# A Trainium2 decoder layer: a cap moved from VectorE to GpSimd, a residual in two halves, bias copies spread, and a query ahead of statistics

## The reference

```python
# attention: R, K, V are linear layers of a mix of the previous and the next token (width 1024)
e  = jnp.exp(jnp.clip(W + K, -20.0, 10.0))          # W = -relu(time_decay) * (t_remaining)
past_attention = jnp.cumsum(e * V, axis=1)
past_energy = jnp.cumsum(e, axis=1)
eu = jnp.exp(jnp.clip(U + K, -20.0, 10.0))
A = shift(past_attention) + eu * V
B = shift(past_energy) + eu
out = (jax.nn.sigmoid(R) * (A / B)) @ Wo.T + bo
# cross attention on ctx
Q = query @ Wq.T + bq ; K = key @ Wk.T + bk ; V = value @ Wv.T + bv
weights = jax.nn.softmax((Q @ K.T + score_matrix) / jnp.sqrt(32.0), axis=-1)
out = (weights @ V) @ Wo.T + bo
```

## Time and profile before

| | us |
|---|---|
| median of 3 runs | 1376.91 |
| lowest, highest | 1374.55, 1377.23 |
| the profiled execution | 1377.34 |
| its span (first to last instruction) | 1375.3 |

### The profile page before, as it was taken

The page is one execution under the profiler, slowest core; times in us unless marked ns, Lnnn a source line. Parts: engine busy times, 40 slices in busy tenths (PEclk is TensorE's granted clock), DMA queues, the critical chain, the costliest instruction groups (busy, mean ns, idle before and its releaser), DMA issues. The chain is left out here.

```text
span 1375.3 us, 19352 instructions
## 1 busy us (share of the span) xinstructions
PE 1327.4 (97%) x6330; PEld 1098.3 (80%) x6330; DVE 1090.5 (79%) x1782; ACT 813.5 (59%) x1555; POOL 634.0 (46%) x558
## 2 busy tenths in 40 slices
PE   5899999999999999999999999999999899999998
PEld 4777887887888878878886778888888778888886
DVE  6999989889899898898988776655555677777774
ACT  5875666656666666666665464444446366666664
POOL 4665344343443433434434544444445455555552
PEclk9999999999999999999999999999999999999999
DMA  9010101001001010010050354444443312222212
GB/s 349 9 30 2 61 31 50 13 31 61 13 17 61 31 58 3 31 61 0 1 222 1 138 210 168 150 146 153 166 147 120 104 59 92 91 91 91 92 62 92
DMA packets 54539, 113.92 MB, mean 83 GB/s; under 512 B 2768, under 2 KB 7120, under 8 KB 52560
## 3 DMA queue, kind: packets, MB, share of 16 engines
q1 hardware_dynamic: 54480, 113.22, 23.2%
HBM read 88.05 MB, written 25.17 MB: 82 GB/s over the span
## 5 line engine op out<-in xcount | busy, mean ns | idle before, releaser
L818 POOL TENSOR_TENSOR a_ss<-a_ss,a_eu 128x512 f32<-128x512 f32 x64 | 82.7, 1293 | 281.4 <-DVE a_ss L630 281.4
L612 DVE SCALAR_TENSOR_TENSOR bank<-bank,k_or_row 128x510 f32<-128x510 f32 x192 | 132.8, 692 | 56.3 <-ACT k_or_row L494 53.3
L823 POOL TENSOR_TENSOR a_sv<-a_sv,a_euv 128x512 f32<-128x512 f32 x64 | 82.8, 1294 | 119.0 <-DVE a_sv L647 119.0
L494 ACT ACTIVATE k_or_row<-bank 128x512 f32<-128x512 f32 x192 | 113.8, 593 | 5.7 <-PE bank L82 0.5
L514 ACT ACTIVATE bank<-bank,a_nbr 128x510 f32<-128x510 f32 x64 | 42.3, 661 | 123.0 <-DVE bank L612 123.0
L401 PE MATMUL bank<-a_wo_hi,a_y_hi 128*128 128x512 f32 x256 | 100.4, 392 | 0.0
L401 PE MATMUL bank<-a_wo_hi,a_y_lo 128*128 128x512 f32 x256 | 99.7, 389 | 0.0
L401 PE MATMUL bank<-a_wo_lo,a_y_hi 128*128 128x512 f32 x256 | 99.6, 389 | 0.0
L1510 POOL TENSOR_TENSOR b_cx_lo<-b_cx,b_cx_hi 128x512 fp32r<-128x512 f32 x32 | 40.6, 1299 | 113.2 <-ACT b_cx_hi L1205 113.2
L827 POOL TENSOR_TENSOR a_y_lo<-a_yy,a_y_hi 128x512 fp32r<-128x512 f32 x64 | 85.6, 1337 | 3.6 <-ACT a_y_hi L537 3.6
L526 ACT ACTIVATE bank<-a_ss 128x512 f32<-128x512 f32 x64 | 38.7, 604 | 74.8 <-DVE a_ss L653 74.8
(11 more groups left out here) (246 smaller groups left out, 4719.4 us busy)
## 6 DMA issues: line engine op xcount, KB each, us to landing
xres<-in_x SPq DMA_DIRECT2D x8, 1024.0 KB, 5.3
x_after_attention<-xres SPq DMA_DIRECT2D x8, 1024.0 KB, 4.3
xin<-x_after_attention SPq DMA_DIRECT2D x8, 1024.0 KB, 5.6
b_ct<-in_ctx_t SPq DMA_DIRECT2D x8, 1024.0 KB, 6.5
b_cx<-in_ctx SPq DMA_DIRECT2D x8, 1024.0 KB, 7.7
xres<-x_after_attention SPq DMA_DIRECT2D x8, 1024.0 KB, 5.7
x_after_cross<-xres SPq DMA_DIRECT2D x8, 1024.0 KB, 4.4
xin<-x_after_cross SPq DMA_DIRECT2D x8, 1024.0 KB, 5.5
```

Source lines behind the costliest of these rows:

```text
L494: sc.activation(u3[:, :, 1:], ps[m][:, :, :], ACT.Copy, scale=MIX[m]).then_inc(left[m], 1)
L612: ve.scalar_tensor_tensor(out=ps[m][:, :, 0:T - 1], in0=ps[m][:, :, 1:T], scalar=1.0 - MIX[m], in1=u3[:, :, 0:T - 1], op0=ALU.mult, op1=AL ...
L818: gp.tensor_tensor(ss3[:, :, 0:T], ss3[:, :, 0:T], eu[:, :, :], ALU.add).then_inc(b_done, 1)
L823: gp.tensor_tensor(sv3[:, :, 0:T], sv3[:, :, 0:T], euv[:, :, :], ALU.add).then_inc(a_done, 1)
```

## The change

Five edits, all in the order of programs or in which engine does a piece of work; no operation is added to the computation.

1. The cap of eu leaves VectorE's `clip` and becomes `clip_own` on GpSimd. VectorE's `weigh_own` now waits for it, and changes places with `mix("r")`.
2. On GpSimd `y_rest` of the group before moves from behind `above` to the front of the group, ahead of `clip_own`.
3. The residual's four additions become two after c = 1 and two in c = 2, between `refine` and `mix("v")`.
4. The bias broadcasts of the last tile are made one each after c = 4, 5 and 6, the two small ones after c = 6.
5. In the cross pass, for the first tile only, ScalarE splits the query high before the context, and VectorE splits the query's rest before and between the statistics of tile 2.

```diff
             def clip(g):
-                ve.tensor_scalar(eu[:, :, :], eu[:, :, :], CLIP_LO, CLIP_HI, ALU.max, ALU.min).then_inc(eu_clip, 1)
                 dve.wait_ge(e_exp, g + 1)
                 ve.tensor_scalar(ee3[:, :, 1:], ee3[:, :, 1:], CLIP_LO, CLIP_HI, ALU.max, ALU.min).then_inc(e_clip, 1)
...
             def weigh_own(g, c):
 
                 dve.wait_ge(edge_v, g + 1)
+                dve.wait_ge(eu_clip, g + 1)
                 wait(dve, a_done, g)
...
-            def wide_biases():
-
-                dve.wait_ge(sh.bias_in, 32)
-                dve.wait_ge(proj["v"], (NT - 1) * HC + KC)
-                for j, b in enumerate((1, 2, 0)):
-                    ve.tensor_copy(sh.bwide[:, j, :].rearrange("p (k r) -> p k r", k=KC),
-                                   sh.bcol[:, b, :].unsqueeze(2).to_broadcast([P, KC, P])
-                                   ).then_inc(bwide_done, 1)
+            def wide_bias(j):
+
+                if j == 0:
+                    dve.wait_ge(sh.bias_in, 32)
+                    dve.wait_ge(proj["v"], (NT - 1) * HC + KC)
+                ve.tensor_copy(sh.bwide[:, j, :].rearrange("p (k r) -> p k r", k=KC),
+                               sh.bcol[:, (1, 2, 0)[j], :].unsqueeze(2).to_broadcast([P, KC, P])
+                               ).then_inc(bwide_done, 1)
+
+            def dot_biases():
+
...
                     if back:
                         refine(g - 1)
+                    if c == 2 and not is_first(i):
+                        residual(i - 1, (2, 3))
                     mix("v", g)
                     clip(g)
                     scan_e(g)
+                    mix("r", g)
                     weigh_own(g, c)
-                    mix("r", g)
                     weigh(g, c)
                     scan_ev(g)
...
                     if c == 1 and not is_first(i):
-                        residual(i - 1, range(SUB))
-                    if is_last(i) and c == HC - 2:
-                        wide_biases()
+                        residual(i - 1, (0, 1))
+                    if is_last(i) and KC <= c < KC + 3:
+                        wide_bias(c - KC)
+                    if is_last(i) and c == KC + 2:
+                        dot_biases()
...
+            def clip_own(g):
+                if isinstance(g, int) and g == 0:
+                    pool.wait_ge(eu_exp, 1)
+                gp.tensor_scalar(eu[:, :, :], eu[:, :, :], CLIP_LO, CLIP_HI, ALU.max, ALU.min).then_inc(eu_clip, 1)
+
...
                         rstd_of(i + 1)
+                    if c > 0 or not is_first(i):
+                        pool.wait_ge(eu_exp, g + 1)
+                        y_rest(g - 1, (c - 1) % HC)
+                    clip_own(g)
                     below(g)
                     above(g)
-                    if c > 0 or not is_first(i):
-                        y_rest(g - 1, (c - 1) % HC)
...
                 for s in range(SUB):
                     exponent(i, s)
-                if ahead:
+                if is_first(i):
+                    q_high(1, 0)
+                    q_high(1, 1)
+                    for k in range(KC):
+                        context_high(1, k)
+                elif ahead:
                     context_high(i + 1, 0)
...
-                if ahead:
+                if is_first(i):
+                    move_rq(1)
+                    q_rest(1, 0)
+                    statistics(2, (0, 1))
+                    q_rest(1, 1)
+                    statistics(2, (2, 3))
+                    dve.wait_ge(st_done, 3 * SUB)
+                    aggregate()
+                elif ahead:
                     move_rq(i + 1)
                     statistics(i + 2)
```

## The result

The changed kernel takes **1476.55 us** (median of 4 runs, 1476.05 to 1476.69) against 1376.73 us for the kernel before on the same chip: a ratio of **1.073**, 95% interval 1.0716 to 1.0743. The forecast was 1435 us with a range up to 1470: right in sign and in the wait it named (before weigh_own), 42 us too small, and, as experiment 8 shows, with the memory going to VectorE and GpSimd in the other order than forecast.

What follows compares the result with a forecast made beforehand. VectorE's round bounds attention, TensorE following with little slack. Rounds +71.2, stretched caps −4.7, residual −5.7, bias −2.8, cross tile +0.3 make +58.3 on 1376.9: 1435 us, range 1395 to 1470.

Steps and rivals of the forecast that it cites:

- About this sum and no more: Attention: relieving VectorE can win only about TensorE's 23 waits for the weighting e·V, 14.4 us in all.
- X: Duration of the cap of eu on GpSimd: 0.94 us taken, 0.77 and 1.30 as ends.
- Rival 3: Cap of eu: two operations per element cost GpSimd twice, X near 1.85, +2.0 us a round, 1492 us; chance 0.03.
- Times 63: Attention: a plain round grows from 10.60 to 11.73 us, +1.13, counted for 63 rounds: +71.2 us.
- rival 1: Attention: y_rest gets the memory before the scan, +0.85 us a round, 1418 us in all; chance 0.22.
- Who is first: VectorE's scan, issued at 4.11 us, gets the memory before GpSimd's y_rest, which asks at 4.26.
- The scan takes turns with GpSimd: Attention: scan and GpSimd work use memory in turn, whole instructions; a 1.23 us scan should end 1.08 after GpSimd.
- Rival 2: Attention: the scan does not contend with GpSimd; rounds last 10.55 us, 1367 us, faster; chance 0.16.
- The rule beside the rows: GpSimd shares SBUF interfaces with VectorE, colliding with two-port modes or two SBUF inputs; by that the change is slower.
- Stretched caps: VectorE's cap of eu takes 0.494 us in the mean, 0.42 alone; moving it saves 4.7 us lost to GpSimd.
- Residual halves: Residual additions after c = 1 and in c = 2: −0.8 us a tile, 7 tiles, −5.7; second half costs 0.3.
- Bias copies: Last tile: spread copies each fit inside VectorE's 1.19 us of idle, the dots add 0.3: −2.8 us.

Runs made afterwards that it cites:

- experiment 8: Changed kernel with a 4-element GpSimd addition ahead of y_rest, so that it starts just behind the scan: 1497.56 us, ratio 1.0878.
- experiment 6: Changed kernel, cap opening GpSimd's group from the second tile on, y_rest back behind `above`, first tile's residual additions earlier: 1360.38 us, ratio 0.9886 to the kernel before.
- experiments 2: Changed kernel with only the upper cap of eu on GpSimd, the lower cap left out: 1452.01 us, ratio 1.054.
- experiment 3: Changed kernel with the cap of eu back on VectorE in its old place, y_rest still in front of `below`: 1426.30 us, ratio 1.036.

## Why the prediction was wrong

**What bounds the kernel: right.** VectorE's round sets attention's pace. "About this sum and no more" (14.4 us) held within the noise: experiment 6 gains 16.0, with an interval of 13.6 to 17.8. TensorE's waits for the weighting fall by 10.8 us there, a 1.9 us wait of a bias product at the end of the pass goes, and TensorE's busy time falls from 1327.4 to 1322.0 us.

**X: the step that failed.** The term "0.23 + 2/3 of 1.07 = 0.94" priced the cap by memory accesses, scaled from a two-input addition, with 1.30 as its dear end. Measured: 1.92 alone, where a copy takes 0.61 and the second operation 0.31. Accesses were the wrong unit. Rival 3 had the size (1.85) and not the reason: the second operation does not double the cost, it adds 0.31 to about 1.61. I gave it 0.03, "against: the small tensor_scalar is cheap": an operation on 4 elements cannot show a price per element. The 0.98 us missing are 63 × 0.98 = 61.7 us; with them the forecast is 1497, above what was measured, and rival 1 is 1480.

**Times 63: wrong too, and hidden by luck.** One plain round stood for all 63. The plain round grew by 2.00 us, which would be 126; attention grew by 101.0, since rounds of other kinds grew less. That 1480 comes so near 1476.6 is therefore partly luck: its round is 0.17 us too short, and it counts that round too often.

**Who is first: wrong, worth 21 us the other way.** I had GpSimd ask for memory 0.35 us after its start; the changed kernel's y_rest wins when issued 0.14 before the scan. That is rival 1 in order (the scan stretched to 2.25, the cap behind it). With its X put right it gives a round of 11.45 + 0.98 = 12.43, measured 12.60. The forecast's order, seen in experiment 8, gives 11.73 + 0.98 = 12.71, measured 12.96. So both chains of the working come within 0.25 us once X is replaced. What they lack is small gaps: weigh_own starts about 0.1 us after the cap, not 0.03, and the cap starts 0.08 after y_rest, not 0.04 before it. The forecast's order would have cost more (1497.6 against 1476.6 us), so this error hid a third of the one in X: in the forecast's own order the miss would have been 62 us, not 42.

**The scan takes turns with GpSimd: right.** "Should end 1.08 after": 1.09, 1.08 and 1.07 us in the changed kernel and experiments 2 and 3. Rival 2, the faster side, is out.

**The rule beside the rows.** The rule of shared SBUF interfaces (the Trainium skill, GPSIMD Engine Reference, section 1) held for the scan too, as this trace shows (2.25 us). The 769 ns for a loop of 512 elements (the Trainium skill, GPSIMD Engine Reference, section 3.1) lie nearer to the copy, measured at 0.62 us, than to the cap of two operations, measured at 1.92.

**Stretched caps, 4.7 us forecast:** VectorE's cap of eu and its lost 4.7 us are gone, but the cap of e, left on VectorE, now takes 30.3 us in all instead of 28.3. In the time this can't be told apart from the rest.

**Residual halves: forecast −0.8 a tile, measured +0.08 alone.** My 0.3 for the second half supposed that the next wait would swallow it; in the kernel before nothing idle follows. In the changed kernel it does more than that: second to third weighting takes 12.03 us there, less than a plain round, since the second half holds the scan back until y_rest is through. The step held only with the cap moved.

**Bias copies: −2.8 forecast, −0.7 measured in the round.** The copies behaved; "the dots add 0.3" was the miss. The product and the copy of its result took 1.24 and 1.27 us, where they had taken 0.15 and 0.23.

**Cross tile: right.** +0.3 forecast, no measurable difference, and the wait reappears at the place named (2.33 us in the changed kernel).

## What to carry over

Price an operation on an engine by a row of the same form and size, or hold the range open to the dearest reading: a small instance of the form shows its fixed cost only. When work moves to an engine that shares memory with the critical one, its place in that queue decides the sign: the same cap costs 50 us behind a y_rest already in front, and the move brings 15 when the cap starts the moment its input is there, beside work that reads PSUM. And one plain round is not every round: add up the kinds of round one by one. Last, a small operation on the critical engine (0.15 us) is not small where it must wait for a whole one of the other (1.25).

## What was not expected of the hardware

- GpSimd on 128x512 fp32: copy 0.62 us, cap with two operations 1.92, addition of two tensors 1.29. This one-input instruction with arithmetic is dearer than the two-input addition.
- The start decides within about a tenth of a microsecond. y_rest won over a scan issued 0.14 us after it; it lost to a cap of e issued 0.01 after it (experiment 3, y_rest 1.59) and to a scan issued 0.01 before it (experiment 8).
- GpSimd's cap seems not to hold the memory throughout. In the changed kernel's third chunk it runs beside the scan, which ends before it does, and both are hardly longer; VectorE and GpSimd there:

```profile
158.19 1.52 DVE L629 TENSOR_TENSOR_SCAN a_ss<-a_mask,a_ee 128x514 f32<-128x514 f32 x1
```

```profile
157.95 1.97 POOL L825 TENSOR_SCALAR a_eu<-a_eu 128x512 f32<-128x512 f32 x1
```

The scan loses 0.29 us, as if the cap let go 0.53 us after its start, and the cap 0.05. That was seen, not tested: no run was made to show when it takes the memory back.
